# A retention layer with mixture of experts: masking in another order, and two sets of transposes moved ahead of a projection

## The reference

```python
x = L0_attn_x                                    # 16 sequences x 256 tokens x 256
q, k, v, g = x @ w_q + b_q, x @ w_k + b_k, x @ w_v + b_v, x @ w_g + b_g     # 8 heads of 32
q, k = theta_shift(q), theta_shift(k)            # rotation by position
sim = einsum('bhnd,bhsd->bhns', q, k / scale) * decay_mask    # 0 where key is after query
ret = einsum('bhns,bhsd->bhnd', sim, v)
r = (ret - mean) / sqrt(var + EPS)               # per token and head
x = layernorm(x + (silu(g) * (r * gn_weight + gn_bias)) @ w_o + b_o)
# top-1 of 8 experts by x @ router_w.T, score = sigmoid of its logit, and a shared expert
shared = silu(x @ shared_gate_w) * (x @ shared_up_w) @ shared_down_w
x = layernorm(x + shared + routed_expert(x * score))
```

## Time and profile before

| | |
|---|---|
| median of 3 runs | 579.01 us (578.83 to 580.04) |
| the profiled execution | 578.61 us, of which the span of its instructions is 576.8 us |
| TensorE, matmuls | 558.0 us busy, 97% of the span |
| VectorE | 391.8 us, 68% |
| ScalarE | 225.6 us, 39% |
| GpSimd | 302.8 us, 52% |
| one step of 3 to 7 on TensorE | 43.1 us (136.54 to 179.68) |

### The profile page before, as it was taken

One profiled execution on the slowest core, in us unless ns is written; L12 is line 12 of the kernel. 1 busy time (PEld: TensorE's weight loads), 2 busy tenths in 40 slices (PEclk: granted clock), 3 DMA queues, 4 the chain that ended last, 5 costly groups with the idle time before them and its releaser, 6 DMA issues.

```text
span 576.8 us, 11184 instructions
## 1 busy us (share of the span) xinstructions
PE 558.0 (97%) x3732; PEld 458.9 (80%) x3732; DVE 391.8 (68%) x826; ACT 225.6 (39%) x403; POOL 302.8 (52%) x311
## 2 busy tenths in 40 slices
PE   7998989999999999999999899999999999999994
PEld 5776778788788788788787687888888888888883
DVE  5888987878877877877876786555644544445543
ACT  3434532553552552552542674133333333333331
POOL 0544592492492492492482555347675555555544
PEclk9999999999999999999999999999999999999998
DMA  7901207203203204501281503822343222222211
GB/s 259 299 6 38 74 2 52 97 1 75 74 1 75 74 2 74 183 2 38 76 362 40 219 19 98 269 57 67 72 84 85 83 74 82 68 80 82 75 47 36
DMA packets 37430, 50.48 MB, mean 88 GB/s; under 512 B 10576, under 2 KB 29520, under 8 KB 37360
## 3 DMA queue, kind: packets, MB, share of 16 engines
q1 hardware_dynamic: 28128, 31.24, 19.0%
q0 software_dynamic: 6048, 15.39, 9.5%
q10 hardware_dynamic: 3200, 3.15, 1.6%
HBM read 36.21 MB, written 13.96 MB: 87 GB/s over the span
## 4 chain that ended last, share of the span: by engine, by line
PE 84%; DVE 5%; issue 4%; POOL 3%; ACT 1%; DMA 0%; POOLq 0%; DVEq 0%; ACTq 0%
PE duo L1484 47%; PE duo L1856 11%; PE duo L1706 6%; PE duo L1540 5%; PE duo L1562 4%; PE duo L1866 3%; PE duo L1696 1%; PE duo L1750 1%; PE duo L1710 1%; PE duo L1644 1%; POOL turned L819 1%; PE duo L1686 1%; PE duo L1602 1%; PE duo L1620 1%; DVE sims L1009 1%
## 5 line engine op out<-in xcount | busy, mean ns | idle before, releaser
L1484 PE MATMUL duo<-w_gu_hi,xsT 128*128 x312 | 107.0, 404 | 0.0
L1484 PE MATMUL duo<-x1T,wsgu 128*128 128x512 f32 x384 | 93.1, 395 | 0.0
L1484 PEld LDWEIGHTS duo<-x1T,wsgu 128*128 128x128 f32 x384 | 70.9, 188 | 15.3
L1433 DVE SCALAR_TENSOR_TENSOR eh<-duo,seat,e_act 128x512 f32<-128x512 f32 x39 | 29.3, 751 | 76.9 <-PE duo L1484 72.0
L1856 PE MATMUL duo<-w_dn,ehT 128*128 x312 | 73.9, 380 | 0.8 <-ACT ehT L802 0.8
L819 POOL TENSOR_TENSOR turned<-turned,swapped 128x1024 f32<-128x1024 f32 x16 | 38.5, 2425 | 67.2 <-DVE swapped L1000 67.2
L938 POOL DMA_INDIRECT out_rows<-of,seat x39 | 39.7, 1018 | 55.8 <-DVE of L1452 52.8
L1484 PEld LDWEIGHTS duo<-w_gu_hi,xsT 128*128 128x128 f32 x312 | 58.6, 188 | 11.3
L1856 PEld LDWEIGHTS duo<-w_dn,ehT 128*128 128x128 f32 x312 | 56.3, 190 | 7.1 <-issue 1.0
L1484 PE MATMUL duo<-w_gu,xsT 128*128 x156 | 60.6, 389 | 0.0
L1009 DVE TENSOR_TENSOR sims<-duo,causal 128x512 f32<-128x512 f32 x64 | 41.2, 686 | 15.9 <-ACT sims L594 15.9
(11 more groups left out here) (171 smaller groups left out, 1131.8 us busy)
## 6 DMA issues: line engine op xcount, KB each, us to landing
w_gu<-L_ffn_gate_up_proj SPq DMA_DIRECT2D x8, 1024.0 KB, 8.3
x_in<-x_t SPq DMA_DIRECT2D x8, 512.0 KB, 6.4
x_res<-L_attn_x SPq DMA_DIRECT2D x8, 512.0 KB, 4.0
xz_d<-zs SPq DMA_DIRECT2D x8, 512.0 KB
xz_d<-x SPq DMA_DIRECT2D x7, 512.0 KB, 4.9
w_dn<-L_ffn_down_proj SPq DMA_DIRECT2D x4, 512.0 KB, 6.2
w_dn<-L_ffn_down_proj ACTq DMA_DIRECT2D x4, 512.0 KB, 8.2
rot<-rotation SPq DMA_DIRECT2D x4, 256.0 KB, 6.9
```

The lines of the kernel that those rows point to most:

```text
L1433: nc.vector.scalar_tensor_tensor(out=eh[:, :], in0=duo[s % 2][:, 1, :], scalar=f32(seat[:, s, :])[:, 2:3], in1=e_act[:, :], op0=ALU.mult, ...
L1484: last = mm(out_, left(a, k), right(b, k), start=start and k == 0 and n == 0, stop=stop and k == kt - 1 and n == len(PASSES) - 1)
```

## The change

It has two parts. In the first, VectorE masks the odd pair of heads of a quad at once when the similarities are there, while ScalarE copies the off-diagonal of the even pair; then they change sides. TensorE now waits for both engines and for both pairs of heads of the quad whose tiles it reuses. This part holds for all steps. In the second part, for steps 3 to 7, `x1_transposes` and `ret_transposes` stand right behind the last values, ahead of `v_project`; the transposed x1 goes to `duo[1]`, so `gate_project`, which writes there, waits for `x1T_lo`. ScalarE does `x1_hi` before `squared`, VectorE does `x1_lo` before the first swap and `v_biased` between the two swaps.

```diff
+        def x1T_early(f):
+            return 0 < f < PAIRS - 2
+
         def x1T_duo(f):
+            if x1T_early(f):
+                return duo[1]
             return duo[0] if f == PAIRS - 2 else x1_duo(f)
...
             def off_diagonal(a, j):
                 act.wait_ge(sig.s_ps, 8 * a + j + 1)
+                if j % 2:
+                    act.wait_ge(sig.s_diag, 8 * a + j)
...
-                    if t not in (2, PAIRS):
+                    if t == 1:
                         squared(a)
                 if has(f):
                     x1_hi(f)
-                    if t in (2, PAIRS):
+                    if t <= PAIRS:
                         squared(a)
...
             def masked(a, quad):
-                for j in range(2 * quad, 2 * quad + 2):
-                    dve.wait_ge(sig.s_off, 8 * a + j + 1)
+                for j in (2 * quad + 1, 2 * quad):
+                    if j % 2:
+                        dve.wait_ge(sig.s_ps, 8 * a + j + 1)
+                    else:
+                        dve.wait_ge(sig.s_off, 8 * a + j + 1)
...
                     products(t, 3)
+                    if t > 2:
+                        x1_lo(f)
                     swap(t, 0)
+                    if t > 2:
+                        v_biased(t)
                     swap(t, 1)
-                    if t != 2:
+                    if t == 1:
                         v_biased(t)
...
                         if kb == 0 and i % 2 == 0 and j >= sim_ring(a):
-                            pe.wait_ge(sig.s_diag, 8 * a + j + 1 - sim_ring(a))
+                            taken = 8 * a + 2 * ((j - sim_ring(a)) // 2) + 2
+                            pe.wait_ge(sig.s_diag, taken)
+                            pe.wait_ge(sig.s_off, taken)
...
             def values(a, n):
                 pe.wait_ge(sig.s_diag, 8 * a + 2 * n + 2)
+                pe.wait_ge(sig.s_off, 8 * a + 2 * n + 2)
...
             def gate_project(t, parts=range(KT)):
+                if x1T_early(t - 2):
+                    pe.wait_ge(sig.x1T_lo, KT * (t - 1))
...
             def x1_transposes(f):
+                elif x1T_early(f):
+                    pe.wait_ge(sig.s_diag, 8 * (f + 2))
+                    pe.wait_ge(sig.s_off, 8 * (f + 2))
...
-                if has(t) and t != 2:
+                if t == 1:
                     v_project(t)
-                if t in (2, PAIRS):
+                if has(f) and t <= PAIRS:
                     x1_transposes(f)
                 if has(a):
                     ret_transposes(a)
-                if has(f) and 2 < t < PAIRS:
-                    x1_transposes(f)
+                if has(t) and t > 2:
+                    v_project(t)
```

More of the change, by code:

```diff
@@ L1350, in _ @@
                 elif has(a):
-                    x1_lo(f)
+                    if t == 2:
+                        x1_lo(f)
                     variance(a)
```

## The result

| | before | after |
|---|---|---|
| median | 578.92 us (4 runs, 578.58 to 580.04) | 583.86 us (4 runs, 583.79 to 584.29) |
| ratio, 95% interval | | 1.0082 [1.0067, 1.0097] |
| the profiled execution | 578.61 us, span 576.8 | 584.29 us, span 582.5 |
| first quad of steps 3 to 8 starts at | 93.41, 136.54, 179.68, 222.81, 265.94, 309.08 | 93.12, 136.97, 181.27, 225.10, 268.94, 312.24 |
| so steps 3 to 7 take | 43.13 or 43.14 each | 43.85, 44.30, 43.83, 43.84, 43.30 |

What follows compares the result with a forecast made beforehand. TensorE, busy 97% of the span, was taken as the bound, so only its gaps could move. Gains of 1.18 us and losses of 3.26 gave net +2.1 on 578.61, with 0.4 for the median: 581.0 us, range 579.0 to 582.6.

Steps and rivals of the forecast that it cites:

- The masks: Second quad's wait for PSUM tiles goes in steps 3, 5, 6, 7: 4 x 0.27 us gained; step 1 gains 0.1.
- The norm behind the copies: Steps 3 to 7: x1's transposes wait 0.11 us for ScalarE's norm, ret's 0.07 to 0.08 more; 0.95 us lost.
- The second shuffle and what hangs on it: Steps 3 to 7: later turn, `rstd` and residual delay `h_low`; `shared_down` waits 0.24 us each, 1.2 us lost.
- Step 3 into step 4: `output_sum` comes 0.8 us later, `project` waits 0.26, masks start late; step 4 loses 0.41 instead of 0.27: 0.14 us.
- Step 8: Pairwise mask release and a later ScalarE norm delay x1's transposes and all after: 0.97 us lost, bounds 0.1 and 1.2.
- The sum: Whole kernel: gains 1.18 us, losses 3.26, net +2.1 us slower, forecast 581.0 us, chance 0.55.
- the collision is as large as in step 2: Rival: turns slip 0.4 us more, `rstd` is late, `shared_down` waits 1.8 us in five steps; 588.9 us, chance 0.10.

Runs made afterwards that it cites:

- xT_low_late: Kernel after the change, with the low part of the next xT moved behind `y_rest` in steps 3 to 6; 581.81 us, ratio 1.0051.
- masks_alone: Kernel before the change, with only the first part (masks and their waits) added; 579.77 us, ratio 1.0017.
- residual_late: Kernel after the change, with GpSimd's residual moved behind the seats in steps 3 to 7; 581.41 us, ratio 1.0045.
- masks_not_last: Kernel before the change, with the first part added for pairs 0 to 6 only, step 8 left as it was; 578.65 us, ratio 0.9993.

## Why the prediction was wrong

- **The masks** (4 x 0.27 gained): right in kind, 0.19 in a step. The second quad takes 1.01 us, 0.07 more than the third of the same step, which has the same waits; what the 0.07 is no row shows. Step 1 gave 0.22, counted from the program's first quad, where I took 0.1.
- **The norm behind the copies** (5 x 0.19): near in size, 5 x 0.13, and wrong in one half. x1's transposes wait 0.18 for the norm, which ends 3.18 us behind the first copy (3.1 forecast); by the router 0.05 of it has come back. And ret's wait for nothing, since the last product was done in time. Without the quicker masks they wait 0.54.
- **The second shuffle and what hangs on it** (5 x 0.24): this is the step that failed, by the size of the term. The place was right: the turns, the residual beside `h_low`, 0.55 us behind it, the wait of `shared_down` (0.24 forecast, 0.21 measured in step 7). But in steps 3 to 6 it is 0.74 us, so 3.2 us in five steps and not 1.2. I had written that `rstd` would take 5.80 us wherever it starts ("it starts at 159.65 ... and ends at 165.45"). It started at 160.31 and took 6.37. The later start is harmless by itself: step 4 as a whole began 0.43 us later, which I had not added, and v_project came at 152.33 and not at 151.7. The 0.55 longer run is the meeting with xT's low part. By my own numbers they came within 0.03 us of each other: `rstd` at 159.65, and xT's low part at 159.50 plus the 0.18 of TensorE's delay, 159.68. I never wrote the second number down. How close it is the last section shows: a power instruction that starts 0.06 us ahead is not slowed. xT_low_late takes that meeting away alone and gives back 2.1 us.
- **Step 3 into step 4** (0.14): 0.27. `project` waits 0.19 for `output_sum`, as said, and the masks behind it start later.
- **Step 8** (0.97): 1.31. The first two releases came as counted. The third does not follow from its own two terms (0.24 and 1.40 in place of 0.75 are 0.89, not the 0.47 that I wrote). Measured, the fourth quad's first copy comes 0.61 later, and its second copy starts 0.97 behind the first where I had 0.78; that is the 0.3. masks_alone shows the same 1.3.
- **The sum**: of the 2.4 us that were missing on TensorE, 2.0 are the `shared_down` term, 0.3 step 8, 0.1 step 4; the other differences cancel to within 0.2. Of the 4.9 us between the medians 4.5 are on TensorE; for the rest, 2.6 us lie between span and time in two of the four runs after, 1.8 in the other two and in the profiled run before, and what fills them no row shows. One more slip: the bounds of my three terms give 579.6 to 582.4 and not 579.9 to 582.3; 583.86 lies outside either.

Of the rivals, "the collision is as large as in step 2" named the right signs: `group_norm`'s second half waiting for `rstd`, and `h_low` behind it. It happened, in four steps. I gave it one chance in ten and a price of 1.8 us a step, because I took step 2's whole wait. Why a step costs 0.74 and not 1.8 no run took apart; step 2 differs in more than the start of `rstd`. And I let the rival hang on turns that slip by another 0.4 us, when the profile had a row for the cause. Here it is, VectorE's of the kernel before, in step 2 and in step 4, with GpSimd's of step 2:

```profile
72.25 1.32 DVE L976 TENSOR_TENSOR xT<-x_in,xT 128x512 fp32r<-128x512 f32 x2
...
75.41 0.69 DVE L1075 TENSOR_TENSOR hT_lo<-s_act,hT_hi 128x512 fp32r<-128x512 f32 x1
...
159.50 1.29 DVE L976 TENSOR_TENSOR xT<-x_in,xT 128x512 fp32r<-128x512 f32 x2 [1.60 <-ACT xT L576]
```

```profile
72.57 6.28 POOL L836 TENSOR_TENSOR rstd<-var_e,minus_half 128x16 f32<-128x16 f32 x2
72.57 3.16 POOL L836 TENSOR_TENSOR rstd<-var_e,minus_half 128x16 f32<-128x16 f32 x1
```

(The second row is the first of the two instructions alone.)

Step 2 had the low part of xT at 72.25 and `rstd` at 72.57, taking 6.28 us; step 4 had `rstd` at 158.37, xT at 159.50, and 5.80 us. In step 2 both of `rstd`'s instructions meet one of VectorE's: the first starts inside xT's low part, the second, at 75.70, inside `h_low` (75.41 to 76.10), and each is some 0.24 us longer. The two durations of one instruction were in the trace, and they differed by what lay beside its start. I moved `rstd` by 1.3 us without looking at what its new start would meet.

## What to carry to other kernels

When a change moves an instruction, look at what lies beside its new place, on the engine it shares SBUF access with, and above all at its new start; if the same instruction has two durations in the trace, find out why before you move it. residual_late shows that moving it out of one collision can put it into the next. Here the instruction that releases the slow engine's chain (a shuffle for GpSimd) belonged ahead of the one that waits for TensorE, the bound (v's bias). A cheap way to price such a chain is a step of the same program that lacks one link, as step 7 here.

## What was not expected of the hardware

- In the ten profiles of this document GpSimd's power instruction `rstd` runs 160 times, 16 in each. 32 of them took 3.14 to 3.48 us and the other 128 took 2.90 to 2.95. All of the 32, and none of the others, started while VectorE ran a 128x512 instruction of two SBUF inputs (the low part of xT, or `h_low`), or within 0.02 us of its start. Each ended 2.76 to 2.79 us behind the end of VectorE's instruction, 0.14 us less than its usual length. So in steps 3 to 6 of the kernel after the 0.55 lies in the first of the two, which meets the whole of a 0.69 us instruction, and in step 2 the 0.48 lies half in each. The rows of the first are, in the kernel after,

```profile
160.31 3.48 POOL L844 TENSOR_TENSOR rstd<-var_e,minus_half 128x16 f32<-128x16 f32 x1
```

and in the kernel before

```profile
158.37 2.93 POOL L836 TENSOR_TENSOR rstd<-var_e,minus_half 128x16 f32<-128x16 f32 x1
```

A lead of 0.06 us is enough. In the kernel after the second of the two started at 163.77 and took 2.91 us, and VectorE's `h_low` behind it took 0.72, 0.04 more than its usual 0.68:

```profile
163.83 0.72 DVE L1086 TENSOR_TENSOR hT_lo<-s_act,hT_hi 128x512 fp32r<-128x512 f32 x1
```

The other way round, VectorE beside the residual, the same 0.14 shows: `h_low`, 0.68 to 0.69 us alone, ended 0.54 to 0.56 behind the residual's end wherever it had started, and the expert's low part in residual_late, 2.29 alone, 2.16 behind it.

The Trainium skill (SBUF — State Buffer, "SBUF: two separate sides") says that whichever of the two engines' instructions starts first has the shared ports for its whole length, and the other is blocked. For the start of a power instruction the traces agree, less the 0.14. For a power instruction that is already running they do not: VectorE's ran beside it in their usual time, but for that 0.04. For the residual the rule holds.

- The clock of TensorE fell to 0.53, next to the lower level of 1.2 GHz, for some 3.6 us in one profiled execution (masks_not_last), in which TensorE was back at work for over a microsecond behind the wait of 1.8 us in step 2 (`shared_down` starts at 84.47, and the clock is at 1.00 until 85.6). The seven other profiles with the same wait had 1.00 there, that of the kernel before among them. With the residual moved out of step 2 the wait of the weight loads is 0.42 to 0.45 us instead of 2.02, and none of 12 runs had a span over 0.5 us above the median of its kernel.
